# A pipelined attention and mixture-of-experts layer: the expert choice and the combine weights' transpose moved one slot later

## The reference, cut to what matters

```python
# attention, 16 heads, keys of 16, values of 64
queries, keys, values = l2norm(queries), l2norm(keys), l2norm(values)
attn = square(relu(einsum('bhid,bhjd->bhij', queries, keys)))
aggr = einsum('bhij,bhjd->bhid', attn, values)
out  = tanh_norm(aggr) * tanh(silu(gates))        # tanh_norm(t) = tanh(|t|) * t / |t|
x    = x + out @ Wout
# experts: 16 of them, 4 groups; 2 groups are kept, then 4 experts of 8
scores  = sigmoid(x2 @ gate_kernel) + gate_bias
combine = top4(scores in the two groups with the largest sum of two scores), normed, * 2.5
y       = sum_e combine[:, e] * ((silu(x2 @ w_gate[e]) * (x2 @ w_up[e])) @ w_down[e])
x       = x + y + shared expert(x2)
```

## Time and profile before

| | |
|---|---|
| median of 3 runs | 830.85 us (829.86 to 833.11) |
| the profiled execution | 831.47 us, of which the span of the trace is 829.5 us |
| busy, share of the span | PE 83%, weight loads 66%, DVE 63%, ACT 52%, POOL 43% |
| mean granted TensorE clock | 0.92 of full speed |
| DMA | 60.94 MB, 73 GB/s over the span |

### The profile page before, as it was taken

One profiled execution on the slowest core, in us unless ns is written; L12 is line 12 of the kernel. 1 busy time (PEld: TensorE's weight loads), 2 busy tenths in 40 slices (PEclk: granted clock), 3 DMA queues, 4 the chain that ended last, 5 costly groups with the idle time before them and its releaser, 6 DMA issues.

```text
span 829.5 us, 16902 instructions
## 1 busy us (share of the span) xinstructions
PE 691.8 (83%) x5160; PEld 545.1 (66%) x5160; DVE 520.7 (63%) x1739; ACT 434.9 (52%) x986; POOL 352.7 (43%) x368
## 2 busy tenths in 40 slices
PE   1576897979979797988979797997979799797785
PEld 1444476858767685867758585876758587676675
DVE  3545667576666748576575757667475856666654
ACT  2466674565646464564646456464655556453211
POOL 2246563644435353544535264453526444363100
PEclk9878998999989898998989899898989999898898
DMA  8994849091835619092562909174371908300000
GB/s 194 132 144 48 131 87 108 14 144 24 124 48 95 72 60 113 6 139 32 94 72 73 98 18 137 24 113 58 79 87 36 128 1 126 40 15 1 8 7 7
DMA packets 72814, 60.94 MB, mean 73 GB/s; under 512 B 8624, under 2 KB 72496, under 8 KB 72752
## 3 DMA queue, kind: packets, MB, share of 16 engines
q1 hardware_dynamic: 72752, 60.26, 49.4%
HBM read 41.37 MB, written 18.87 MB: 73 GB/s over the span
## 4 chain that ended last, share of the span: by engine, by line
PE 57%; DVE 25%; issue 9%; ACT 4%; DMA 2%; DVEq 1%; POOL 1%; SPq 1%; ACTq 0%; POOLq 0%
PE ps_a L503 11%; PE ps_f L365 8%; PE ps_f L428 7%; PE ps_f L367 6%; PE ps_f L366 6%; PE ps_f L447 5%; PE ps_s L474 5%; PE ps_f L424 4%; DVE norms_m L741 2%; PE ps_f L407 2%; DMA qkt<-qk_rows 2%; DVE it L852 2%; PE ps_f L418 2%; DVE norms_t L661 2%; DVE norms_t L662 2%
## 5 line engine op out<-in xcount | busy, mean ns | idle before, releaser
L334 POOL TENSOR_TENSOR p<-r 128x512 f32<-128x512 f32 x256 | 262.5, 1046 | 392.4 <-ACT r L603 392.4
L603 ACT ACTIVATE r<-ps_s 128x512 f32<-128x512 f32 x256 | 138.5, 596 | 81.0 <-PE ps_s L474 79.8
L503 PE MATMUL ps_a<-p,v 128*64 128x256 f32 x1024 | 143.5, 396 | 3.4 <-DVE big L897 2.2
L897 DVE TENSOR_TENSOR big<-ps_a,wt 128x256 f32<-128x256 f32 x128 | 53.7, 420 | 73.7 <-ACT big L612 51.1
L503 PEld LDWEIGHTS ps_a<-p,v 128*64 128x64 f32 x1024 | 64.4, 138 | 41.7 <-POOL p L334 2.7
L852 DVE TENSOR_TENSOR it<-ps_f,it 128x256 f32<-128x256 f32 x144 | 59.1, 420 | 44.0 <-ACT it L595 41.0
L595 ACT ACTIVATE it<-ps_f 128x256 f32<-128x256 f32 x144 | 55.2, 383 | 50.1 <-PE ps_f L367 47.7
L418 PE MATMUL ps_f<-ident,cs 128*32 128x128 f32 x32 | 9.2, 387 | 83.8 <-DVE cs L787 83.8
L447 PE MATMUL ps_f<-wdown,it 128*128 128x128 f32 x576 | 71.2, 279 | 2.9 <-DVE it L869 1.7
L869 DVE TENSOR_TENSOR it<-ps_f,it 128x512 f32<-128x512 f32 x64 | 44.0, 690 | 44.8 <-PE ps_f L424 44.3
L447 PEld LDWEIGHTS ps_f<-wdown,it 128*128 128x128 f32 x576 | 68.4, 195 | 4.5 <-DVE it L869 1.8
(11 more groups left out here) (153 smaller groups left out, 1607.2 us busy)
## 6 DMA issues: line engine op xcount, KB each, us to landing
qk_rows<-qk_parts SPq DMA_DIRECT2D x16, 1024.0 KB, 4.4
qkt<-qk_rows SPq DMA_DIRECT2D x64, 256.0 KB, 9.5
qkt<-qk_rows SPq DMA_DIRECT2D x128, 128.0 KB, 8.9
x_in<-in_L_attn_tokens SPq DMA_DIRECT2D x16, 128.0 KB, 2.2
x_res<-in_L_attn_tokens SPq DMA_DIRECT2D x16, 128.0 KB, 14.4
out<-o_sb SPq DMA_DIRECT2D x16, 128.0 KB, 14.2
big<-in_L_attn_Wqg SPq DMA_DIRECT2D x1, 640.0 KB, 4.2
big<-in_L_attn_Wkv SPq DMA_DIRECT2D x1, 640.0 KB, 5.3
```

What stands on the lines that cost most here:

```text
L334: pool.tensor_tensor(p[h % 4][:], r[h % 2][:], r[h % 2][:], ALU.mult).then_inc(probs_done, 1)
L503: last = pe.matmul(ps_a[k % 2][64 * e:64 * e + 64, 0:N], v[q][:, t, h * DV:(h + 1) * DV], p[h % 4][:, t * N:(t + 1) * N], start=(t == 0), ...
L603: act.activation(r[h % 2][:], ps_s[h % 2][:], ACT.Relu).then_inc(relu_done, 1)
L897: dve.tensor_tensor(aw[ap][:, pair, :], ps_a[pair % 2][:, 0:N], wt[ap][:, pair, :], ALU.mult)\
```

## The change

In the table, cT moves from the head of slot 3 to its end, behind rT, and cB 0 from the end of slot 3 into slot 4, behind gu 8. The fillers between thereby move up in places and change banks. On VectorE, gate_up 5 moves up to slot 2; route_experts moves from slot 2 to slot 3, behind head_scales, gated_heads and gate_up 6; value_scales comes after it and gate_up 7; scale_hidden 0 moves behind gate_up 8 in slot 4. ScalarE follows the table.

```diff
@@ -45,8 +45,8 @@
         [("P", "v", 0), ("F", "lg", 0), ("P", "v", 1), ("F", "gu", 0), ("F", "gu", 1)],
         [("N", "ones", 0), ("P", "v", 2), ("F", "gu", 2), ("N", "nT", 0), ("P", "v", 3)],
         [("F", "gu", 3), ("P", "g", 0), ("F", "gu", 4), ("F", "gu", 5)],
-        [("F", "cT", 0), ("F", "gu", 6), ("P", "g", 1), ("F", "gu", 7), ("O", "rT", 0), ("F", "cB", 0)],
-        [("O", "rB", 0), ("O", "rB", 1), ("F", "gu", 8), ("O", "rB", 2), ("O", "rB", 3), ("P", "g", 2)],
+        [("F", "gu", 6), ("P", "g", 1), ("F", "gu", 7), ("O", "rT", 0), ("F", "cT", 0)],
+        [("O", "rB", 0), ("O", "rB", 1), ("F", "gu", 8), ("F", "cB", 0), ("O", "rB", 2), ("O", "rB", 3), ("P", "g", 2)],
         [("F", "cB", 1), ("L", "xT", 0), ("O", "y", 0), ("F", "cB", 2), ("O", "y", 1), ("F", "cB", 3)],
         [("L", "qk", 0), ("P", "g", 3), ("F", "y2", 0), SKIP],
         [("L", "qk", 1), ("F", "y2", 1), ("O", "x2T", 0), SKIP],
@@ -937,29 +937,27 @@
                             gate_up([3])
                         gated_heads(k)
                         if F:
-                            gate_up([4])
-                            route_experts(link_f, fb)
-                            link_f.end()
+                            gate_up([4, 5])
                     if k == 3:
                         if O:
                             head_scales(link_o, b)
                             link_o.end()
+                        gated_heads(k)
                         if F:
-                            gate_up([5])
-                        gated_heads(k)
+                            gate_up([6])
+                            route_experts(link_f, fb)
+                            link_f.end()
+                            gate_up([7])
                         if P_on:
                             value_scales(link_p, s + 1, rq2[pq])
                             link_p.end()
-                        if F:
-                            gate_up([6, 7])
                     if k == 4:
-                        if F:
-                            scale_hidden([0])
                         if O:
                             scale_heads([0, 1])
                         gated_heads(k)
                         if F:
                             gate_up([8])
+                            scale_hidden([0])
                         if O:
                             scale_heads([2, 3])
                         if L_on:
```

## The result

| | before | changed |
|---|---|---|
| median | 831.38 us (20 runs, 829.86 to 833.8) | 827.81 us (20 runs, 824.63 to 834.93) |
| ratio to before | | 0.9964, 95% interval 0.9949 to 0.9979 |
| profiled execution | 831.47 us, span 829.5 | 830.53 us, span 828.8 |
| mean granted clock of the profiled execution | 0.920 | 0.930 |

The change makes the kernel 3.6 us faster, 0.4%; the forecast was 11.5 us, down to 819.4. The runs of the changed kernel also scatter more, and with the clock: those with a mean granted clock of 0.942 took 824.6 to 825.4 us, those with 0.924 took 832.1 to 832.9, the one with 0.920 took 834.9.

The account below looks back on a forecast made before the run. TensorE was taken as the main bound (57% of the chain), losing 5.36 us a step waiting and 2.1 to half clock. 2.1 - 1.35 = 0.75 us over 14 steps, 10.5, plus 1, gave 11.5: 819.4 us, range 803 to 833.

Parts of the forecast that it names:

- The sum for cT: End of slot 3: VectorE's summed chain up to the combine weights lets cT start at 282.3, 7.37 us after slot 2's values.
- the value between the bounds: VectorE before cT: L780 gets in at GpSimd's seam, the cast is held; cT at 282.3, between 281.8 and 282.8.
- The waits: TensorE in slots 3 and 4: gu 6 waits 1.5 us, rT 0.7, cT 2.8, g 2 0.45.
- What can be won is just the 2.1 us that the half clock costs: TensorE, each step: with equal idle time, only the 2.1 us lost to half clock behind the wait can be gained.
- the idle time is the same: TensorE, each step: four waits after the change sum to 5.4 us against one of 5.36 before.
- I take 1.35 on average: TensorE, slot 4: half clock still falls in most steps and costs 1.35 us a step, leaving 0.75 gain.
- the 1 us summed for the last two steps: Last two steps: less VectorE work ahead of the choice than TensorE work ahead of cT; some 0.5 us gained each.
- the short stretch: TensorE, slot 4: half clock as in the step at 186, busy 2.4 to 3.4 us, costing 1.0 to 1.5 us.
- the long form: TensorE behind cT: half clock near 7 us, costing up to 2.9 us, of which g 2's wait returns 0.4.
- (2): Rival, TensorE: the wait only moves, idle sum equal, half clock costs 2.1 us again; 831 us, 827 to 835; chance 0.29.
- (1): Rival, TensorE: the clock stays up in every step, gaining 30 us, to 801 us; chance 0.13.
- (3): Rival, slots 4 and 5: later cT, about 282.6 or beyond, and long half clock on busy work; slower, 843 us; chance 0.11.

Follow-up runs that it names:

- experiment 3: Changed kernel with route_experts back in slot 2 behind gate_up 5, and gate_up 6 ahead of gated_heads 3; TensorE's table stays changed: 799.98 us.
- experiment 4: Changed kernel with one 128x512 memset on VectorE ahead of route_experts, so the choice comes later: 837.16 us.
- experiment 5: Changed kernel with four extra matmuls on TensorE ahead of cT, filling the hole only in part: 811.72 us.
- experiment 1: Changed kernel with ten extra matmuls, results overwritten, filling TensorE's hole ahead of cT: 802.99 us.
- experiment 2: Kernel before the change with seventeen extra matmuls filling TensorE's hole ahead of cT: 803.23 us.
- experiment 6: On top of experiment 3, rT and gu 8 at the head of slot 4; VectorE takes gated_heads 4 and gate_up 8 before scale_heads 0: 788.16 us.
- 7: Kernel of experiment 3 with eight extra matmuls on TensorE ahead of rT: 788.51 us.
- 8: Kernel of experiment 6 with six extra matmuls on TensorE ahead of cT: 783.96 us.

## Why the prediction was wrong

**The work and the waits: right.** Each moved step lies where it was put. The sum for cT was 7.37 us after slot 2's values, and 7.33 was measured; the holds by GpSimd (L780 in the seam, the cast to the end of the second squaring, L832 free) came as taken from the earlier trace rows; the value between the bounds was the right one. The waits were forecast at 1.5, 0.7, 2.8 and 0.45 us and measured at 1.36, 0.53, 2.65 and 0.18. The four waits are 4.7 us in all and not 5.4; cT was on time all the same, because it starts by VectorE's chain and not by the waits ahead of it. For the cast, which no row before showed beside GpSimd, the row of 0.95 us now agrees with the Trainium skill, "SBUF — State Buffer", section "Who interferes with whom", which has copies and casts among the work of VectorE that can need the pair of ports shared with GpSimd.

**No gain from order: right, but partly by luck.** "What can be won is just the 2.1 us that the half clock costs" held: filled, the two kernels are 0.2 us apart, and the cost of the clock before was 28.2 us, against the 2.1 x 14 = 29 of the text. Its premise, "the idle time is the same", did not: the waits fell by 0.6 us a step. As the filled kernels are equally long, TensorE's work must have grown by as much, a term that the sum has at nothing; the two cancelled.

**The clock's cost after the change: wrong.** This is the step that failed, the term "I take 1.35 on average". Measured it is 24.8 us in the whole kernel, 1.8 us in each of 14 steps; with 18.9 forecast, the 6 us between them are most of the miss of 8. The other 2 are that the clock's cost before was 28.2 us and not 29.4, and that the 1 us summed for the last two steps does not show: filled, the whole kernels differ by 0.2. The forecast took the short stretch as the usual form, and its witness was the one step at 186, although 13 of the 14 steps before had the long form. 1.35 lies inside the short form's own range of 1.0 to 1.5, and so leaves next to no room for long steps. The profiled executions show the size. In the 14 steps the clock was at half for 92.2 us before and for 78.5 after, less by 14; but TensorE was busy for 65.3 of the former and for 68.9 of the latter. Before, the first part of each stretch lay on the standstill, where it costs nothing; now more of it lies on work. At 42% that is 27.4 us before and 28.9 after, 2.1 us a step. Put into the sum in place of 1.35 it gives some 830 us for the profiled execution, which took 830.5. (That the medians give 1.8 fits the clocks of the runs: the profiled execution has 0.930, the middle of the 20 runs 0.935.)

When the long form comes is known only in part. In the changed kernel, where the clock fell more than 0.3 us ahead of the start of the waiting cT (9 steps), it was back 6.8 us after its fall; where it fell less than 0.3 us ahead of it or behind it (5 steps), 3.4 us after. The profiled executions of experiments 3 (with rT, which waits there), 4 and 5 follow this too. The kernel before does not: at 186 the clock fell 0.7 us ahead of cT and was back after 3.4 us. That is the very step which the forecast took as its witness. How many steps would be long could not be read from the rows of the kernel before.

**The rivals.** (2), "the wait only moves", was what came, though not for nothing: 3.6 us. (1) did not come by itself: with standstills of 2.65 to 3.0 us ahead of cT the half clock came in 14 of 14 steps. Its condition, a clock that stays up, was made by hand in experiment 1 and gave 803, where the text has 801. (3) came only in another kernel, when the choice was pushed later still, in experiment 4, at 837 instead of 843. Its point, a cT later than the sum by a few tenths, was near: 6.4 us of waiting turn the change from 0.4% faster into 0.6% slower than the kernel before.

## What to carry to other kernels

A wait that is cut in pieces is not yet a gain: add up the idle time of the pieces, count some extra work for each new stop (an estimate from the rows of experiments 1 and 2: 0.6 us for three stops here, 0.2 each), and ask of the clock where its half-speed stretch will now lie; a stretch that used to begin on a standstill and now lies on work costs as much although it is shorter. Two cheap experiments help: before any reordering is tried, fill the hole with useless matmuls, which prices the clock alone; after it, undo the part of the change on one engine, which here was worth over seven times what the change brought. When a cost has two forms in the trace, count the forms over all steps before taking one of them.

## What the runs showed of the hardware

How often the half clock came can't be told from the longest standstill ahead of the transpose alone: 5.0 to 5.8 us, 14 of 14 steps; 3.2 us (experiment 4) and 2.65 to 3.0 us, 14 of 14; 2.2 to 2.5 us, but 3.1 in the last step (experiment 3), 8 of 14; 1.2 to 1.5 us behind filled work (experiment 5), 6 of 14; 1.6 to 1.9 us, but 2.5 in the last step (experiment 6), 1 of 14. What puts all ten kernels in order, but for one step, is everything that TensorE stands still around the transpose. The gaps over 0.1 us from 9 us ahead of its start to 8 us behind it, added up, are on average of the 14 steps:

| kernel | standing still, us a step | half clock in steps of 14 |
|---|---|---|
| before; experiment 4; changed | 5.4; 5.4; 4.9 | 14; 14; 14 |
| experiments 3; 5; 6 | 3.9; 3.6; 3.3 | 8; 6; 1 |
| experiments 1; 7; 8 | 2.4; 2.0; 1.8 | 0; 0; 0 |
| experiment 2 | 1.4 | 1 |

This order was found afterwards, and no run was made to test it.

Useless work can pay: over 140 to 680 us the busy time of TensorE rose from 477 to 522 us when the hole of the kernel before was filled, and the kernel was 3.4% faster. A VectorE instruction held by GpSimd got in at the seam between two squarings that follow each other without a gap: L780 did in all 14 steps from 137 to 748 us (0.63 to 0.79 us instead of 0.18), and the cast behind it was held to the end of the second. The two lines in the changed kernel (least/median/largest in ns):

```profile
L780 DVE TENSOR_TENSOR nn<-nn,bound x16: 181/631/785, 98.2 to 784.4; 128x32 f32<-128x32 f32 x16
```

```profile
L785 DVE CAST split_hi<-nn x16: 182/953/955, 98.4 to 784.6; 128x32 fp32r<-128x32 f32 x16
```
